# The last group of a lower-triangle Gram kernel: its row turns, copies and stores rearranged, and rows packed four quarters sooner

## The reference

```python
Z = jnp.einsum('bnd,bmd->bnm', inputs, inputs)   # inputs (2048, 64, 256) float32
li, lj = jnp.tril_indices(64, k=-1)
y = Z[:, li, lj]                                  # (2048, 2016) float32
```

## Time and profile before

| | us |
|---|---|
| median of three runs | 418.18 |
| the profiled execution, its own time | 417.85 |
| span of its trace | 416.1 |
| TensorE busy | 377.6 |
| VectorE busy | 364.5 |
| ScalarE busy | 178.8 |
| GpSimd busy | 199.9 |
| TensorE's last matmul ends | about 400.5 |
| from there to the end of the span | 15.6 |

### The profile page before, as it was taken

The page is one execution under the profiler, slowest core; times in us unless marked ns, Lnnn a source line. Parts: engine busy times, 40 slices in busy tenths (PEclk is TensorE's granted clock), DMA queues, the critical chain, the costliest instruction groups (busy, mean ns, idle before and its releaser), DMA issues.

```text
span 416.1 us, 68691 instructions
## 1 busy us (share of the span) xinstructions
PE 377.6 (91%) x33024; PEld 370.4 (89%) x33024; DVE 364.5 (88%) x224; ACT 178.8 (43%) x829; POOL 199.9 (48%) x981
## 2 busy tenths in 40 slices
PE   4469999999999999999999999999999899899940
PEld 4469999999999999999999999999999899898940
DVE  3438899999999999999999998999979799797964
ACT  0011134434555434554345543455544445444465
POOL 1000084664818283564828183563808356182783
PEclk9559999999999999999999999999999999999985
DMA  8259999999999999999999999999999999995218
GB/s 325 87 181 425 426 419 425 418 423 421 420 421 423 423 421 421 422 420 423 380 423 399 388 419 411 403 380 415 347 425 338 422 382 358 392 326 247 68 50 199
DMA packets 21178, 151.01 MB, mean 363 GB/s; under 512 B 2592, under 2 KB 2720, under 8 KB 4768
## 3 DMA queue, kind: packets, MB, share of 16 engines
q1 hardware_dynamic: 18752, 135.26, 81.3%
q10 hardware_dynamic: 2400, 15.48, 9.9%
HBM read 134.22 MB, written 16.52 MB: 362 GB/s over the span
## 4 chain that ended last, share of the span: by engine, by line
PE 55%; DMA 31%; DVE 5%; issue 5%; ACT 2%; ACTq 0%; DVEq 0%
PE bank_set L252 55%; DMA x_in<-x_dram 31%; DVE x_turned L198 4%; ACT packed_rows L120 1%; DVE row_halves L215 1%; ACT packed_rows L126 1%; DVE x_turned L221 0%; ACTq L137 0%; ACT products L279 0%; DVEq L197 0%; ACTq L68 0%; DVEq L214 0%; ACTq L294 0%; ACTq L270 0%
## 5 line engine op out<-in xcount | busy, mean ns | idle before, releaser
L252 PE MATMUL bank_set<-x_turned 32*64 32x64 f32 x33024 | 377.6, 236 | 22.7 <-issue 11.9
L252 PEld LDWEIGHTS bank_set<-x_turned 32*64 32x64 f32 x33024 | 370.4, 132 | 29.8 <-issue 22.6
L198 DVE STREAM_TRANSPOSE x_turned<-x_in 128x2048 f32<-128x2048 f32 x128 | 292.0, 2290 | 41.2 <-PE bank_set L252 18.0
L131 POOL COPY packed_rows<-row_halves 32x60 f32<-32x60 f32 (+30 forms) x961 | 196.4, 206 | 209.2 <-DVE row_halves L215 171.6
L279 ACT COPY products<-bank_set 128x512 f32<-128x512 f32 (+1 forms) x91 | 68.6, 760 | 208.6 <-PE bank_set L252 189.3
L215 DVE STREAM_TRANSPOSE row_halves<-products 128x1024 f32<-128x1024 f32 x64 | 77.1, 1207 | 3.2 <-ACT products L279 2.7
L120 ACT COPY packed_rows<-row_halves 128x32 f32<-128x32 f32 (+30 forms) x481 | 62.8, 220 | 0.0
L126 ACT COPY packed_rows<-row_halves 128x128 f32<-128x128 f32 x256 | 56.9, 300 | 4.3 <-issue 3.0
L279 ACT ACT_TABLE_LOAD x1 | 1.3, 1283 | 19.9 <-PE bank_set L252 19.9
L131 DVE COPY packed_rows<-row_halves 32x2 f32<-32x2 f32 (+30 forms) x31 | 3.4, 187 | 0.0
L120 POOL COPY packed_rows<-row_halves 128x2 f32<-128x2 f32 (+14 forms) x15 | 2.3, 210 | 0.1
## 6 DMA issues: line engine op xcount, KB each, us to landing
x_in<-x_dram SPq DMA_DIRECT2D x128, 1024.0 KB, 17.3
y_dram<-packed_rows ACTq DMA_DIRECT2D x30, 504.0 KB, 8.1
y_dram<-packed_rows SPq DMA_DIRECT2D x2, 380.0 KB, 3.9
y_dram<-packed_rows SPq DMA_DIRECT2D x2, 124.0 KB, 3.6
```

The costliest lines, as they stand in the source:

```text
L131: return copy(packed_rows[first:first + BLOCK, group % 2, :, at + BLOCK:at + i], row_halves[first + BLOCK:first + HALF, i, :, 0:i - BLOCK])
L198: nc.vector.transpose(x_turned[:, j].rearrange("p c b s (h u n v) -> p u v (c b s h) n", h=ROWS // BLOCK, u=PAIRS, v=PAIR), x_in[:, k]).th ...
L252: done = nc.tensor.matmul(bank_sets[s][side * HALF:(side + 1) * HALF, g, at, :].rearrange("r (n u v) -> r u n v", u=PAIRS, v=PAIR), rows, ...
```

## The change

The last group is dealt with by code of its own in more places, and one constant that holds for all groups changes.

- `PACK_LAG` goes from 23 to 19: every quarter is packed four quarters sooner in ACT's order.
- The last group's row turns go to `last_halves`, which is a view of the first two buffers of the input ring, and no more to `row_halves`. So they no longer wait for the packing of group 14. They are cut otherwise: one transpose of 128x2048 (the half of the group's batches that its first four tiles hold, all rows) after tile 123 is kept, then four of 128x512 (the other half, a piece each) after the last keep.
- DVE carries one side across, as before, and then packs rows 1 to 15. POOL carries the other side, and then packs rows 24 to 31. ACT packs rows 32 to 63 and 16 to 23.
- SP stores group 14, both sides, and side 0 of the last group; ACT stores side 1 of the last group (`store_last`). Each of them stores the long rows first and then the short ones.

```diff
-    PACK_LAG = 2 * PIECE_LAG + 1
+    PACK_LAG = 2 * PIECE_LAG - 3
+    LAST_HOME = (GROUPS * PIECES - 2) * 4 + 2
...
+        last_halves = x_in[:, 0:ROWS * KEPT // (JOINED * DIM)].rearrange(
+            "p k (i h j) -> p (k i) h j", h=RUNS, j=BLOCK)
...
+        def store_last(engine, side):
+            group, long_rows = GROUPS - 1, first_column(BLOCK)
+            engine.wait_ge(packed_home, group * PIECES + LONG_PIECES)
+            engine.wait_ge(packed_across, (group + 1) * LONG_PIECES)
+            engine.wait_ge(last_carried, 1)
+            store(engine, group, slice(long_rows, PACKED), [side])
+            engine.wait_ge(packed_home, GROUPS * PIECES - 1)
+            engine.wait_ge(last_packed, 2)
+            store(engine, group, slice(0, long_rows), [side])
...
+            sync.wait_ge(packed_home, (GROUPS - 1) * PIECES)
+            sync.wait_ge(packed_across, (GROUPS - 1) * LONG_PIECES)
+            store(sync, GROUPS - 2, slice(0, PACKED))
+            store_last(sync, 0)
...
-            rows = piece_rows(PIECES - 1)
-            for i in range(1, rows.stop):
+            rows = piece_rows(PIECES - 2)
+            for i in range(rows.start + PIECE // 2, rows.stop):
                 last = pack_short(nc.gpsimd.tensor_copy, GROUPS - 1, i)
...
-            for n in range(turned_rows, GROUPS * PIECES):
+            for n in range(turned_rows, (GROUPS - 1) * PIECES):
                 turn_rows(n)
+            for run in range(RUNS):
+                lap, j = place((GROUPS - 1) * GROUP_TILES + (run + 1) * GROUP_TILES // RUNS - 1)
+                s = set_of(j)[0]
+                dve.wait_ge(kept[s], (lap + 1 + s) * LAP)
+                if run < RUNS - 1:
+                    turn_last_rows(run, slice(0, ROWS))
+                else:
+                    for piece in range(PIECES):
+                        turn_last_rows(run, piece_rows(piece)).then_inc(rows_turned, 1)
...
+            for i in range(1, piece_rows(PIECES - 1).stop):
+                last = pack_short(nc.vector.tensor_copy, GROUPS - 1, i)
+            last.then_inc(last_packed, 1)
...
-            for n in range(n, (GROUPS * PIECES - 1) * 4):
-                if n == (GROUPS - 1) * PIECES * 4:
-                    store_whole(GROUPS - 2)
+            for n in range(n, LAST_HOME):
                 pack(n)
+            store_last(act, 1)
```

More of the change, by code:

```diff
@@ L116, in wait_packed_free, with halves @@
                 engine.wait_ge(stored[group % 2], group // 2 * STORES)
+        def halves(group):
+            return last_halves if group == GROUPS - 1 else row_halves
         def pack_short(copy, group, i):
             at = first_column(i)
-            return copy(packed_rows[:, group % 2, :, at:at + i], row_halves[:, i, :, 0:i])
+            return copy(packed_rows[:, group % 2, :, at:at + i], halves(group)[:, i, :, 0:i])
         def pack_long_pair(copy, group, i):
@@ L125, in pack_long_pair @@
             two = packed_rows[:, group % 2, :, at:at + 2 * i].rearrange("p h (w c) -> p h w c", w=2)
-            return copy(two[:, :, :, 0:BLOCK], row_halves[:, i:i + 2].rearrange("p w h j -> p h w j"))
+            return copy(two[:, :, :, 0:BLOCK], halves(group)[:, i:i + 2].rearrange("p w h j -> p h w j"))
         def carry_across(copy, group, i, side):
@@ L131, in carry_across, with store @@
             return copy(packed_rows[first:first + BLOCK, group % 2, :, at + BLOCK:at + i],
-                        row_halves[first + BLOCK:first + HALF, i, :, 0:i - BLOCK])
-        def store(engine, group, columns):
+                        halves(group)[first + BLOCK:first + HALF, i, :, 0:i - BLOCK])
+        def store(engine, group, columns, sides=range(SIDES)):
             rows = y[group * GROUP:(group + 1) * GROUP, columns].rearrange("(h q s) c -> s q h c", h=RUNS, s=SIDES)
-            for side in range(SIDES):
+            for side in sides:
                 engine.dma_start(rows[side],
@@ L154, in _ @@
                 load(t)
[L156 to L163, removed]
+            sync.wait_ge(packed_home, (GROUPS - 1) * PIECES)
+            sync.wait_ge(packed_across, (GROUPS - 1) * LONG_PIECES)
+            store(sync, GROUPS - 2, slice(0, PACKED))
+            store_last(sync, 0)
             for b in range(2):
                 groups = (GROUPS - b + 1) // 2
-                sync.wait_ge(stored[b], (groups + (1 if group % 2 == b else 0)) * STORES)
+                sync.wait_ge(stored[b], (groups + (1 if (GROUPS - 1) % 2 == b else 0)) * STORES)
         @block.gpsimd
@@ L183, in _ @@
             pool.wait_ge(packed_across, GROUPS * LONG_PIECES)
-            pool.wait_ge(rows_turned, GROUPS * PIECES)
-            rows = piece_rows(PIECES - 1)
-            for i in range(1, rows.stop):
+            pool.wait_ge(rows_turned, GROUPS * PIECES - 1)
+            rows = piece_rows(PIECES - 2)
+            for i in range(rows.start + PIECE // 2, rows.stop):
                 last = pack_short(nc.gpsimd.tensor_copy, GROUPS - 1, i)
@@ L218, in turn_rows, with turn_last_rows @@
                     rows_turned, 1)
+            def turn_last_rows(run, rows):
+                return nc.vector.transpose(
+                    last_halves[:, rows, run].rearrange("p i (n u v) -> p i u n v", u=PAIRS, v=PAIR),
+                    products[:, (GROUPS - 1) % KEPT_RING, rows, run * BLOCK:(run + 1) * BLOCK])
             for j in range(BLANK):
@@ L227, in _ @@
                     turned_rows += 1
-            for n in range(turned_rows, GROUPS * PIECES):
+            for n in range(turned_rows, (GROUPS - 1) * PIECES):
                 turn_rows(n)
+            for run in range(RUNS):
[7 more added lines that the diff above has]
+                        turn_last_rows(run, piece_rows(piece)).then_inc(rows_turned, 1)
             wait_packed_free(dve, GROUPS - 1)
-            dve.wait_ge(rows_turned, (GROUPS - 1) * PIECES + LONG_PIECES)
+            dve.wait_ge(rows_turned, GROUPS * PIECES)
             for i in range(BLOCK + 1, ROWS):
@@ L300, in pack @@
                         last = pack_long_pair(nc.scalar.copy, group, i)
-                if quarter == 3:
+                if quarter == 3 or n == LAST_HOME - 1:
                     last.then_inc(packed_home, 1)
```

## The result

The changed kernel takes 414.68 us (median of 15 runs, 412.12 to 416.24); the kernel before took 416.93 us in its 15 (415.8 to 419.54). The ratio is 0.9933, 95% interval 0.9918 to 0.9947: faster by 0.67%, 2.8 us (2.2 to 3.4 by the interval), which is within 1%. The medians differ by 2.25 us. The forecast was 416.3 us, 1.9 us less than before, and within 1%. Of the 1.6 us by which 416.3 lies above the measured time, 1.25 us are the base: the forecast started from 418.18 us, the median of three runs, and over 15 runs that median is 416.93.

What follows compares the result with a forecast made beforehand. DMA and TensorE were taken to run neck and neck, with the gain in the tail's chain into the drain. The profiled 417.85 us less 1.9 gave 415.95, or 416.3 for the median from 418.18; range 413.7 to 418.2.

Steps and rivals of the forecast that it cites:

- The forecast's case: Tail: the drain of groups 14 and 15 starts 1.9 us sooner, stays unbroken, and the end is 1.9 us earlier; chance 0.60.
- Store of group 14: After the last keep: 19 copies left to ACT instead of 33, so SP issues this store 1.9 us earlier.
- Row turns: Group 15 on DVE: one big transpose of 2.2 us before the last keep ends, then four small ones, 2.5 us together.
- Copies: Group 15: DVE's carries 3.36 us, POOL's 4.8; long rows issued at 407.1 by SP, 407.7 by ACT, short ones at 408.8.
- The 2.8 us on DVE are then hidden by the drain: Tail: DVE's row turns end 2.8 us sooner, hidden except what keeps group 15 from being late for the drain.
- rival E: Group 15's row turns: the change doesn't shorten them; 1.5 us of delay would leave 417 us; chance 0.05.
- 0.8 us of that cost nothing: Group 15's row turns: the drain lets 0.8 us of delay in them cost nothing.
- The drain's pace with two sides: Tail stores on two queues: one after the other at 229 GB/s or together at 412; the first was taken.
- Rival B: Tail drain: the two sides drain together at 412 GB/s, 3.9 us less, 414.3 us by the median; chance 0.20.
- Rival C: End of the loads: group 13's earlier store delays the last load, costing 0.5 to 1 us, leaving 417 us; chance 0.10.
- Rival D: Ahead of keeps of set 0: ACT waits for row turns and TensorE stands, 420 us or more; chance 0.05.
- Less lag in the other groups, taken as nothing: All groups before the tail: each is stored one keep sooner; cost and gain taken as nothing.

Runs made afterwards that it cites:

- e2: The changed kernel with PACK_LAG back at 23, all else as changed; tail 14.3 us, ratio 0.9972 to the kernel before.
- e6: The changed kernel with the big transpose of the last group's first half also waiting for the last keep; tail 15.2 us, ratio 0.9977 to the kernel before.
- e8: The changed kernel with DVE carrying across after two small transposes, turning the other two behind that; tail 12.3 us, ratio 0.9912 to the kernel before.
- e4: The changed kernel with group 14's store on two queues, SP side 0 and ACT side 1; tail 12.4 us, ratio 0.993 to the kernel before.
- e9: The changed kernel with PACK_LAG 17 instead of 19; tail 12.9 us, ratio 0.994 to the kernel before.
- e7: The changed kernel with the edits of both e4 and e8; tail 11.9 us, ratio 0.9909 to the kernel before.
- e3: The changed kernel with all of the last group's stores on SP, none on ACT; tail 13.2 us, ratio 0.9958 to the kernel before.
- e10: The changed kernel with PACK_LAG 15 instead of 19; tail 13.0 us, ratio 1.0015 to the kernel before.
- e1: The kernel before with PACK_LAG 19 instead of 23, nothing else; tail 15.2 us, ratio 0.9984 to the kernel before.
- e12: e8 with SP storing group 14's side 1 first and side 0 second; tail 12.9 us, ratio 0.991 to the kernel before.

## Why the prediction was right, and where its steps were off

The forecast's case, a drain that starts 1.9 us sooner and stays unbroken, is what happened; 1.9 us were forecast and 2.3 measured in the tail. That it stays unbroken was a near thing: the long rows were issued 0.65 us later than forecast (see the copies below), and 0.3 us of margin were left. To that extent the close number is luck, and the 0.4 us by which the drain is shorter were not forecast.

- *Store of group 14*: 1.9 us sooner, forecast and measured (2.76 for 4.70 us). Right; e2 takes the lag away and the store is at 4.7 again.
- *Row turns*: 2.2 and 2.5 us forecast, 2.27 and 2.49 measured. Right. The big one sits ahead of the last keep.
- *Copies*: too cheap. DVE's carries took 3.87 us, not 3.36, and POOL's 4.91, not 4.8, with both at work at once from the start; that one slows the other is not shown. SP issued the long rows 7.2 us behind the last keep, not 6.5 (ACT 7.2, forecast 7.1), the short ones 8.6, not 8.2.
- *"The 2.8 us on DVE are then hidden by the drain"*, and in rival E *"0.8 us of that cost nothing"*: this failed. The cover, from the first packet of the last group (8.0 us behind the last keep) to the end of group 14's last (8.3), was 0.3 us, not 0.8, and in e6 2.2 us of delay cost 2.0 to 2.3. Also e8: copies that end 0.6 us sooner shorten the tail by 0.6 to 0.9 us with no hole to close. The drain and the copies are bounds at the same time in the changed kernel: e4 speeds up the drain of group 14 and gains 0.5 to 0.8 us, with the copies where they were, but e9, which only starts the drain sooner, gains nothing.
- *The drain's pace with two sides*: the mis-sized term. I took 229 GB/s against 412 and let the trace's 238 decide. That was a misreading: by 408.6 as many packets of group 14 had left as one side has (64), so the window behind it held the other side alone and said nothing on two at once. For the changed kernel the number was near all the same (281 and 231 GB/s). But it isn't a property of the engines: 310 to 320 GB/s in e4 and e7, 303 in e8, 324 in e2. The rule of the Trainium skill ("DMA: Bandwidth & Descriptors", Rules for kernel authors), that transfers to disjoint halves serialize, does not hold here: 1.03 MB took 3.3 us as two sides at once and 4.7 us one behind the other. The port map that the Trainium skill gives in "SBUF — State Buffer" (Door 1) fits better: 194 to 206 GB/s with one side, for its 218, though two sides together came to 324, not to twice as much.
- *Rival B*: two sides in flight together are faster (e4, e2), but in this kernel the split of the last group gave none of it (e3). SP and ACT issue the long rows at the same moment, 7.17 and 7.19 us, but side 1's first packet leaves 1.3 us behind side 0's, at 9.3.
- *Rival C*: refuted for this kernel. Group 13's store is issued at 387.53, with the last loads still on one engine (share 0.06, 23 GB/s). In the next window the share is 1.07: the other engines do the store, and the load packets of the one keep coming 0.31 us apart. The turns of the last tiles have no pause before them:

```profile
390.07 4.46 DVE L215 STREAM_TRANSPOSE x_turned<-x_in 128x2048 f32<-128x2048 f32 x2
```

  and TensorE runs through its last six tiles:

```profile
381.37 17.44 PE L288 MATMUL bank_set<-x_turned 32*64 32x64 f32 x1536 [0.36 <-DVE x_turned L215]
```

  At lag 17 its mechanism is there: the 0.64 us wait of e9.

- *Rival D*: its mechanism is real at lag 15 (e10: 3.6 us of pauses, ratio 1.0015 against 0.993) and absent at 19.
- *Less lag in the other groups, taken as nothing*: right, as far as it can be told. e1 shows 0.3 us in the tail, and a ratio of 0.9984, 0.7 us, whose interval (0.1 to 1.3 us) takes in both.

The best versions are e7 and e8, with tails 1.0 to 1.3 and 0.6 to 0.9 us shorter than the changed kernel's; their ratios, 0.9909 and 0.9912, have intervals that overlap with its own.

## What to carry to other kernels

When two things meet at the end of a chain, here a drain and the copies that feed it, price each with the other in place: the two halves of this change gave 0.3 and 1.2 us alone and 2.3 us together, in tails that repeat to 0.3 us. Before you call work "hidden", compare when it ends with when its cover ends, and take the margin, not the length of the cover. If stores are made of partition slices as here, try to issue slices of different halves at the same moment on different queues: here that made 3.3 us of 4.7 for one group, and 0.5 to 0.8 us of the tail.

## What the hardware showed unexpectedly

- The pace of a store depended on what else was in flight: a packet of 6 KB from side 0 took 0.42 us in the changed kernel, 0.25 us when it met packets of side 1, and 0.37 us when it met its own side (e12).
- At the end of the loads one DMA engine of sixteen is behind the others: from 386.5 the share is 0.06, and 0.00 only from 392.3; in the changed kernel it is 0.06 at 387.6.
- An ACT store issued by itself at the end sent its first packet after 0.83 us (group 14 in the kernel before). Issued at the same moment as one on SP's queue it took 1.5 us (group 14 in e4) to 2.1 us (changed kernel); SP's own took 0.8 us in both cases.
